# The first stage's pieces in a new order, the first expert weights loaded during it, and gathers spread over the first cross-attention tile

## The chip, the cores and the metric

One core of one Trainium2 chip runs the whole program in one launch. The metric is the device time in microseconds (us) from launch to end; the kernel before was timed three times, and one further execution was recorded by the hardware profiler. TensorE is called PE here, VectorE DVE, ScalarE ACT, GpSimd POOL and SyncE SP.

## The reference

All data is float32. `x` is (32, 32, 512), that is 1024 tokens, 8 tiles of 128; `ctx_1024` is (32, 257, 512), one context of 257 rows for each group of 32 tokens.

```python
x = x + _L0_xattn_ref(_layernorm(x), ctx_1024, ctx_1024, ctx_1024)   # (gelu(x ctx^T) * (x ctx^T)) ctx
x = x + _L0_attn_ref(_layernorm(x), w_qkv, w_proj, q_norm_w, k_norm_w)  # RMS norm, rope, causal, 16 heads
x = x + _L0_ffn_ref(_layernorm(x), gate_w, gate_b, w1, b1, w2, b2)   # 32 experts, top 2, capacity 77
x = x + _L1_xattn_ref(_layernorm(x), ctx_1024, Wq, bq, Wk, bk, Wv, bv, Wo, bo)
x = x + _L1_attn_ref(_layernorm(x), ...)     # group norm, decayed linear attention, SiLU MLP
x = x + _L1_ffn_ref(_layernorm(x), w_freq_real, w_freq_imag, bias)   # ifft(fft(x) @ w), as one real matrix
```

The router of the third line is

```python
probs = softmax(xt @ gate_w + gate_b); top_w, top_i = top_k(probs, 2)
pos_all = cumsum(one_hot(top_i.reshape(-1)), axis=0) - 1   # place of each token within its expert
xe = zeros(E, C, D).at[flat_e, pos_d].add(x_rep, mode='drop')
he = gelu(einsum('ecd,edf->ecf', xe, w1) + b1, approximate=False)
ye = einsum('ecf,efd->ecd', he, w2) + b2
```

## The kernel before

The program is written engine by engine, with semaphores set by hand, and each engine runs its instructions strictly in the order in which they stand. It has three stages.

The first stage (`phase_a`, lines 359 to 378) goes over the 8 tiles. A tile's work is cut into pieces: `gated(i)` is the first line of the reference (layer norm, its transposes at L1361, the products with the context at L1368 and L1384, the next layer norm and its transposes at L1333); `scored(i)` makes queries, keys and values (the 512 wide matmuls of L1323), norms and turns them on DVE (L963 to L979, with a root on POOL at L550), transposes them (L1407) and multiplies them to scores (L1414); `attended(i)` is the softmax, the product with the values (L1427), the projection (L1323) and the third layer norm; `routed(i)` gives the gate's logits (L1323, 32 wide). Each engine has a generator for each piece, and `interleave` strings them by the letters of `PLAN_A` (g, a, z, w for gated, scored, attended, routed), so that several tiles are under way; tiles 2 to 6 are the turns of a hardware loop.

Then `PLAN_B` joins the last tiles with `spectral` (the 257 wide matmuls of L1323, first half of the real matrix of the last reference line, after `folds` on DVE at L945) and with `route(0)`, the router for tiles 0 to 5; `route(1)` does it for tiles 6 and 7. POOL writes the token rows to the experts' places in DRAM by 16 indirect DMAs (L591, the scatter). Behind that PE does a small reordering of biases (L1460) and the second half of the spectral matrix, waits for `m_sb`, transposes the first expert's rows (L1477) and begins the experts.

SP (lines 395 to 540) issues the loads. The weights of an expert are `w1` and `w2`, 4 MiB each, in a ring of two places each; the first stage's own buffers lie in the same memory. Before, SP waited for the last gate matmul (`gate_ps`) and loaded w1 and w2 of expert 0; then it waited for the scatter and loaded the first two experts' rows; then it waited for the spectral matrix and loaded w1 of expert 1.

The second stage is the 32 experts (hidden layer L1488, transposes L1496, result L1506). The third, `phase_c`, goes over the 8 tiles again: `head`, `cross` (cross-attention, 4 contexts a tile: scores L1593, softmax on DVE at L1220 and ACT at L823, transposes L1608, values, keys of the next context), and `tail` (the rest). Ahead of each tile it adds the two gathered expert outputs of every token (`add_expert`, L1166). POOL gathers tile 0 ahead of the stage and the other seven tiles, 14 indirect DMAs, in one row behind the first layer norm (`gather_others`, L664); DVE waits for all of them once and adds them in pieces during tile 0's cross-attention (`other_tiles`, L1295).

## Time and profile before

| what | value |
|---|---|
| median of 3 runs | 2064.54 us (2060.41 to 2065.12) |
| the profiled execution | 2075.67 us |
| its span, first to last instruction | 2073.9 us |
| PE busy | 1934.6 us, 93% of the span |
| DVE, ACT, POOL busy | 704.7, 556.9, 196.9 us |
| mean granted PE clock | 0.970 |
| DMA | 374.95 MB, mean 181 GB/s |

"Busy" is the time in which an engine had an instruction at work. In the rows below a timeline line gives start and length in us, the engine, the line of the kernel, the operation, output<-input, the number of instructions merged, and in brackets the idle time before it with the engine that ended it. The granted clock 1.00 is PE's full 2.4 GHz and 0.50 is 1.2 GHz. The profiled execution lies 11.13 us above the median of the runs. By time the stages are: first stage and routing from 0 to about 336 us, experts to about 1098 us, the rest to the end.

### The profile page before, as it was taken

How to read it: one execution, taken by the hardware profiler on the slowest of the kernel's cores; microseconds unless marked ns; L12 is line 12 of the kernel's file. 1: busy time of each engine (PE TensorE's matmuls, PEld its weight loads, DVE VectorE, ACT ScalarE, POOL GpSimd, SP SyncE). 2: the span in 40 equal slices, each digit the busy share in tenths (PEclk: the TensorE clock that was granted, in tenths of full speed). 3: DMA queues.
4: the chain of work that ended last, by engine and by line, in shares of the span. 5: the costliest groups of instructions: out<-in, count | busy, mean ns of one | idle time of the engine just before them, and what ended most of it. 6: DMA issues, size and time to landing. Idle time of an engine off the chain costs nothing.

```text
span 2073.9 us, 37462 instructions
## 1 busy us (share of the span) xinstructions
PE 1934.6 (93%) x15676; PEld 981.9 (47%) x15676; DVE 704.7 (34%) x1536; ACT 556.9 (27%) x1123; POOL 196.9 (9%) x182
## 2 busy tenths in 40 slices
PE   5789777999999999999996999999999999999977
PEld 2444453333333333333333657565666656575543
DVE  2666671121111211112223433434323333344323
ACT  1333311222222222222211234233333333242321
POOL 1122221000000000000003000000000000000000
PEclk9999988999999999999998999999999999999988
DMA  9643228999999999999976020100000000000000
GB/s 338 221 163 144 79 73 344 396 396 387 382 388 375 380 362 379 379 375 379 367 280 207 22 102 22 27 21 27 12 26 22 21 27 22 17 22 27 11 1 11
DMA packets 86295, 374.95 MB, mean 181 GB/s; under 512 B 7782, under 2 KB 25702, under 8 KB 53432
## 3 DMA queue, kind: packets, MB, share of 16 engines
q1 hardware_dynamic: 79544, 355.71, 44.9%
q0 software_dynamic: 6656, 17.77, 2.4%
q8 instruction: 83, 1.36, 0.3%
q14 instruction: 12, 0.10, 0.0%
HBM read 357.73 MB, written 16.45 MB: 180 GB/s over the span
## 4 chain that ended last, share of the span: by engine, by line
PE 85%; issue 4%; ACT 3%; SPq 3%; DMA 2%; DVE 2%; POOL 1%; another core or an unknown queue 0%; POOLq 0%; DVEq 0%; ACTq 0%
PE ps L1323 38%; PE ps L1506 16%; PE ps L1488 16%; PE ps L1713 3%; PE ps L1496 2%; PE ps L1608 1%; PE ps L1514 1%; DMA arena<-in_ctxT 1%; ACT arena L685 1%; PE ps L1384 1%; PE ps L1593 1%; DMA xe_rows<-arena,uidx 1%; PE ps L1634 1%; SPq L432 1%; PE ps L1477 1%
## 5 line engine op out<-in xcount | busy, mean ns | idle before, releaser
L1323 PE MATMUL ps<-arena 128*128 128x512 f32 (+3 forms) x3120 | 893.6, 442 | 38.0 <-ACT arena L685 10.0
L1323 PEld LDWEIGHTS ps<-arena 128*128 128x128 f32 x3120 | 529.1, 193 | 372.6 <-issue 296.7
L1506 PE MATMUL ps<-arena 128*32 128x512 f32 x3072 | 373.6, 594 | 0.0
L1488 PE MATMUL ps<-arena 128*32 128x512 f32 x3072 | 363.3, 595 | 0.7 <-issue 0.6
L550 POOL TENSOR_TENSOR arena<-arena 128x1 f32<-128x1 f32 (+3 forms) x80 | 129.2, 1615 | 1103.2 <-DVE arena L913 643.7
L1121 DVE COPY arena<-ps 128x512 f32<-128x512 f32 x96 | 66.4, 691 | 482.7 <-PE ps L1506 482.7
L1488 PEld LDWEIGHTS ps<-arena 128*32 128x32 f32 x3072 | 109.3, 109 | 225.4 <-issue 225.4
L1506 PEld LDWEIGHTS ps<-arena 128*32 128x32 f32 x3072 | 100.4, 109 | 198.1 <-issue 195.6
L783 ACT ACTIVATE arena<-ps 128x512 f32<-128x512 f32 x96 | 57.3, 597 | 352.5 <-PE ps L1488 352.5
L813 ACT ACTIVATE arena<-ps,arena 128x257 f32<-128x257 f32 x128 | 60.7, 477 | 202.8 <-PE ps L1323 202.8
L1220 DVE TENSOR_REDUCE arena<-ps 128x1 f32<-128x257 f32 x128 | 54.2, 423 | 122.5 <-PE ps L1593 112.7
L789 ACT ACTIVATE arena<-arena 128x512 f32<-128x512 f32 x96 | 58.3, 631 | 127.2 <-DVE arena L1128 127.1
L607 POOL DMA_DIRECT2D y_rows<-arena x32 | 16.8, 526 | 744.4 <-DVE arena L1136 744.4
L823 ACT ACTIVATE arena<-ps,arena 128x257 f32<-128x257 f32 x128 | 60.6, 476 | 92.7 <-DVE arena L1221 78.1
L830 ACT ACTIVATE arena<-ps 128x512 f32<-128x512 f32 x64 | 34.9, 595 | 172.7 <-PE ps L1608 172.5
L1213 DVE TENSOR_TENSOR arena<-ps,arena 128x512 f32<-128x512 f32 x64 | 43.9, 689 | 76.6 <-PE ps L1323 76.5
L1128 DVE TENSOR_TENSOR arena<-ps,arena 128x512 f32<-128x512 f32 x96 | 60.3, 684 | 20.0 <-PE ps L1496 20.0
L1136 DVE TENSOR_TENSOR arena<-ps,arena 77x512 f32<-77x512 f32 x32 | 22.0, 688 | 117.7 <-PE ps L1514 117.7
L1713 PE MATMUL ps<-arena 128*128 128x512 f32 x128 | 61.5, 625 | 0.0
L1496 PEld LDWEIGHTS ps<-arena 128*128 128x128 f32 x384 | 41.3, 140 | 26.0 <-issue 26.0
L1496 PE MATMUL ps<-arena 128*128 128x128 f32 x384 | 48.9, 277 | 0.0
L1608 PE MATMUL ps<-arena 128*128 128x128 f32 x256 | 34.1, 277 | 13.1 <-DVE arena L1226 13.1
(198 smaller groups left out, 1323.8 us busy)
## 6 DMA issues: line engine op xcount, KB each, us to landing
arena<-in_w SPq DMA_DIRECT2D x64, 4096.0 KB, 13.8
arena<-in_ctxT SPq DMA_DIRECT2D x8, 2056.0 KB, 7.9
arena<-in_ctxT SPq DMA_DIRECT2D x32, 514.0 KB, 3.6
arena<-in_ctx SPq DMA_DIRECT2D x8, 2048.0 KB
xe_rows<-arena SPq DMA_DIRECT2D x8, 616.0 KB
arena<-in_b POOLq DMA_DIRECT2D x32, 154.0 KB, 7.5
arena<-xe_rows SPq DMA_DIRECT2D x32, 154.0 KB
y_rows<-arena POOLq DMA_DIRECT2D x32, 154.0 KB, 6.2
```

The costliest lines, as they stand in the source:

```text
L550: pool.tensor_tensor(dst, src, half_sb[:, 0:src.shape[-1]], ALU.pow).then_inc(done, 1)
L783: act.activation(h_sb[:, t, :].rearrange("p (c f) -> p c f", c=HB), ps[:, t, :].rearrange("p (f c) -> p c f", c=HB), ACT.Copy).then_inc(h_ ...
L789: act.activation(hT[s][:, t], hT[s][:, t], ACT.Gelu).then_inc(hT_rdy, 1)
L813: act.activation(kT_c[:, m, :], ps[:, bK(m), 0:S], ACT.Identity, bias=bk_sb[:, m:m + 1], scale=1.0).then_inc(k_ev, 1)
L823: act.activation(P_c[:, g, 0:S], ps[:, bS(g), 0:S], ACT.Exp, bias=nmx[:, g:g + 1], scale=SCALE, accum_out=smc[:, g:g + 1]).then_inc(exp_c, 1)
L1121: dve.tensor_copy(yp_sb[:, t, :], ps[:, ST + t, :]).then_inc(yp_out, 1)
L1128: TT(hT[s][:, t].rearrange("p c (n u) -> p c n u", n=HB), ps[:, t, :].rearrange("p (c n u) -> p c n u", c=HB, n=HB), bc(b.unsqueeze(3), P, ...
L1323: ins = pe.matmul(dst, lhsT, rhs, start=(n == 0), stop=(n == len(pairs) - 1))
L1488: ins = pe.matmul(ps[q4[n], t, :], xeT[s][:, k, q4[t]], w1_sb[s][:, k, n * D:(n + 1) * D], start=(k == 0), stop=(k == KD - 1))
L1496: ins = pe.transpose(ps[:, t, chunk(c)], h_sb[:, t, chunk(c)], id_sb)
L1506: ins = pe.matmul(ps[q4[n], ST + t, :], hT[s][:, t, c, q4[n]], w2_sb[s][:, n * HB + c, :], start=(c == 0), stop=(c == HB - 1))
L1713: ins = pe.matmul(ps[:, w.b7, :], w.hT2[:, f, :], fw2_sb[:, f, :], start=(f == 0), stop=(f == FT2 - 1))
```

## The change

Four things change together.

1. The first stage gets a new order. The first layer norm and its transposes are cut off `gated` as `lead`, and run two tiles ahead. Values are made ahead of queries and keys; the scores' matmuls move from `scored` to `attended`, behind the next tile's value matmuls. The rope on DVE works on the raw queries and keys, and the root mean square's factor is multiplied in last, so rope no longer waits for POOL. PSUM banks change with it: transposes of queries and keys use banks 4 and 5, the scores bank 3 (6 in the last tile), the routing bank 3 (7 in the last two tiles). `folds` is cut in two parts, one in the last `scored`, one in the last `attended`.
2. The first stage's buffers are laid out so that w1 of expert 0 can be loaded when the last tile's queries and keys are turned (`qkT_rdy`), and w1 of expert 1 and w2 of expert 0 when the last projection is done (`proj_ps`).
3. The bias reordering and the second half of the spectral matrix become a piece `matrix`, which is interleaved with `route(1)`. The first two experts' rows are loaded by POOL, not SP, behind the scatter.
4. The gathers of tiles 1 to 7 are issued in four groups (4, 4, 4 and 2), each when the softmax of one context of tile 0 is done and the group before has landed; DVE adds each tile where it stands in a list.

PE, first stage, the whole order of one turn (the unrolled one of scored(1)), before; L1368 and L1384 are the products with the context, L1323 with 512 columns queries, keys, values and the projection:

```order
L1323 MATMUL ps<-arena 128x512 x12
L1361 MATMUL ps<-arena 128x128 x4
L1368 MATMUL ps<-arena 32x257 x16
L1427 MATMUL ps<-arena 32x128 x16
L1375 MATMUL ps<-arena 128x128 x2
L1375 MATMUL ps<-arena 1x128
L1384 MATMUL ps<-arena 32x512 x12
L1323 MATMUL ps<-arena 128x512 x4
L1407 MATMUL ps<-arena 128x128 x8
L1333 MATMUL ps<-arena 128x128 x4
L1414 MATMUL ps<-arena 32x128 x16
```

and now (L1418 is L1361 of before, L1427 is L1368, L1434 is L1375, L1443 is L1384, L1389 is L1333, L1468 is L1407, L1478 is L1414, L1490 is L1427, L1379 is L1323):

```order
L1379 MATMUL ps<-arena 128x512 x4
L1478 MATMUL ps<-arena 32x128 x16
L1379 MATMUL ps<-arena 128x512 x8
L1427 MATMUL ps<-arena 32x257 x16
L1490 MATMUL ps<-arena 32x128 x16
L1434 MATMUL ps<-arena 128x128 x2
L1434 MATMUL ps<-arena 1x128
L1443 MATMUL ps<-arena 32x512 x12
L1379 MATMUL ps<-arena 128x512 x4
L1389 MATMUL ps<-arena 128x128 x4
L1468 MATMUL ps<-arena 128x128 x8
L1418 MATMUL ps<-arena 128x128 x4
```

The scores stood behind the transposes of their own queries and keys; now the next tile's four value matmuls stand between them. The transposes of `lead` stand last, for the tile after next.

PE, end of the first stage and the way to the experts, before (L1450 are the router's counts, L1460 the bias reordering, L1323 with 257 columns the spectral matrix, L1477 the first expert's rows):

```order
L1450 MATMUL ps<-arena 128x192 x2
L1427 MATMUL ps<-arena 32x128 x16
L1323 MATMUL ps<-arena 128x512 x4
L1323 MATMUL ps<-arena 128x257 x16
L1333 MATMUL ps<-arena 128x128 x4
L1323 MATMUL ps<-arena 128x32 x4
L1450 MATMUL ps<-arena 128x64 x2
L1460 MATMUL ps<-arena 32x128 x16
L1323 MATMUL ps<-arena 128x257 x20
L1477 MATMUL ps<-arena 128x77 x4
```

and now:

```order
L1516 MATMUL ps<-arena 128x192 x2
L1490 MATMUL ps<-arena 32x128 x16
L1379 MATMUL ps<-arena 128x512 x4
L1379 MATMUL ps<-arena 128x257 x16
L1389 MATMUL ps<-arena 128x128 x4
L1379 MATMUL ps<-arena 128x32 x4
L1525 MATMUL ps<-arena 32x128 x16
L1379 MATMUL ps<-arena 128x257 x10
L1516 MATMUL ps<-arena 128x64 x2
L1379 MATMUL ps<-arena 128x257 x10
L1551 MATMUL ps<-arena 128x77 x4
```

The bias reordering and ten of the twenty matmuls now stand ahead of the second counts.

POOL, from the last stores of expert results to the third stage's loop, before (L623 are the gathers, L550 the roots of the layer norms of tiles 0 and 1):

```order
L607 DMA y_rows<-arena 77x512 x2
L623 DMA arena<-y_rows,uidx 128x512 x2
L550 TENSOR_TENSOR arena<-arena 128x1
L623 DMA arena<-y_rows,uidx 128x512 x14
L550 TENSOR_TENSOR arena<-arena 128x1
```

and now:

```order
L623 DMA y_rows<-arena 77x512 x2
L639 DMA arena<-y_rows,uidx 128x512 x2
L558 TENSOR_TENSOR arena<-arena 128x1
L639 DMA arena<-y_rows,uidx 128x512 x8
L558 TENSOR_TENSOR arena<-arena 128x1
L639 DMA arena<-y_rows,uidx 128x512 x6
```

The root of tile 1's layer norm now stands behind the second of the four groups.

The core of the diff:

```diff
-        rA = Region(ring_off[0][0], 2 * RW)
+        rA = Region(ring_off[0][0], RW)
...
+        rA = Region(ring_off[0][1], RW)
...
-        rM = Region(ring_off[1][0], RW)
         KH, HF = KD // 2, D // 2
-        ATr, ATi, tmpM = rM.take(KH, D), rM.take(KH, D), rM.take(2, HD)
+        ATr, tmpM = rM.take(KH, D), rM.take(2, HD)
+        ATi = view(WORDS - KH * D, KH, D)
...
-        PLAN_A = "gzawgawgzgagzaga"
-        PLAN_B = "zwwrmrzzrm"
+        PLAN_A = "hazagawzgawgzagazh"
+        PLAN_B = "wzwrmrzzzrm"
...
+        def bA(i):
+            return 6 if isinstance(i, int) and i == NT - 1 else 3
+
+        def bR(i):
+            return 7 if isinstance(i, int) and i >= NT - 2 else 3
...
+        def phase_a(eng, lead, gated, scored, attended, routed, spectral, my, per, route, matrix):
+
+            run(lead(0))
             run(gated(0))
-            interleave(PLAN_A, a=scored(0), g=gated(1))
-            interleave(PLAN_A, a=scored(1), g=gated(2), z=attended(0))
-            with eng.Fori(2, NT - 1) as i:
+            run(lead(1))
+            interleave(PLAN_A, a=scored(0), g=gated(1), h=lead(2))
+            interleave(PLAN_A, a=scored(1), g=gated(2), h=lead(3), z=attended(0))
+            with eng.Fori(2, NT - 2) as i:
                 if my is not None:
                     my.loop(i, per, 2)
-                interleave(PLAN_A, a=scored(i), g=gated(i + 1), z=attended(i - 1), w=routed(i - 2))
+                interleave(PLAN_A, a=scored(i), g=gated(i + 1), h=lead(i + 2), z=attended(i - 1), w=routed(i - 2))
             if my is not None:
-                my.leave(NT - 1)
+                my.leave(NT - 2)
+            interleave(PLAN_A, a=scored(NT - 2), g=gated(NT - 1), z=attended(NT - 3), w=routed(NT - 4))
             interleave(PLAN_A, a=scored(NT - 1), z=attended(NT - 2), w=routed(NT - 3))
             interleave(PLAN_B, z=attended(NT - 1), w=routed(NT - 2), m=spectral, r=route(0))
             run(routed(NT - 1))
-            run(route(1))
+            interleave("rsrsrs", r=route(1), s=matrix)
...
-            sp.wait_ge(gate_ps, NT)
+            sp.wait_ge(qkT_rdy, 5 * NT)
             load_w1(0, 0)
+            sp.wait_ge(proj_ps, NT)
+            sp.dma_start(w1_sb[1], rows(w1[1])).then_inc(w1_in[1], 16)
             load_w2(0, 0)
-            sp.wait_ge(scattered, 16 * 2 * NT)
-            for s in range(2):
-                load_rows(s, s)
             sp.wait_ge(m_sb, 2 * KD)
...
-            load_w1(1, 1)
...
+            pool.wait_ge(scattered, 16 * 2 * NT)
+            for s in range(2):
+                pool.dma_start(xe_sb[s][0:CAP, :], xe_dram[s * CAP:(s + 1) * CAP, :]).then_inc(xe_first, 16)
...
-            def gather_others():
-                for i in range(1, NT):
-                    gather(i)
-                return {}
-
-            phase_c(pool, head, cross, tail, None, None, gather_others)
+            def other_tiles():
+                yield
+                for b in range(NB):
+                    pool.wait_ge(pn_rdy, (HG + 1) * (b + 1))
+                    if b > 0:
+                        pool.wait_ge(gathered, 32 * 2 * b)
+                    for i in range(2 * b + 1, min(2 * b + 3, NT)):
+                        gather(i)
+                    for _ in range((2, 4, 4, 5)[b]):
+                        yield
+
+            def first_tile():
+                return {"t": other_tiles()}
+
+            phase_c(pool, head, cross, tail, None, None, first_tile)
...
+            def moments(a, src, w=None):
+                stats_rdy = ln_stats[a] if w is None else w.ln_stats
                 dve.drain()
                 dve.bn_stats(stats, src)
                 dve.drain()
                 my.step(dve.bn_aggr(mv, stats))
                 TS(veps, mv[:, 1:2], LN_EPS, None, ALU.add).then_inc(stats_rdy, 1)
+
+            def normed(a, src, dst, n, done=None, w=None):
...
+            def folds(part):
+                even, odd, w, w_in = ((We_r, Wo_r, Wr_sb, Wr_in), (We_i, Wo_i, Wi_sb, Wi_in))[part]
+                dve.wait_ge(w_in, 16)
+                TT(even[:, :, 1:HF], w[:, :, 1:HF], w[:, :, D - 1:HF:-1], ALU.add).then_inc(W_fold, 1)
+                TT(odd[:, :, 1:HF], w[:, :, 1:HF], w[:, :, D - 1:HF:-1], ALU.subtract).then_inc(W_fold, 1)
+                dve.tensor_copy(even[:, :, 0:1], w[:, :, 0:1]).then_inc(W_fold, 1)
+                odd, sign = ((Wo_i, -1.0), (Wo_r, 1.0))[part]
+                TS(odd[:, :, 0:1], w[:, :, HF:HF + 1], sign, None, ALU.mult).then_inc(W_fold, 1)
...
-                my.step(TT(qkn, ps[:, 4:6, :].rearrange("p a (h d) -> p (a h) d", h=H),
-                           bc(rs.unsqueeze(2), P, 2 * H, DH), ALU.mult))
+                yield
                 v4 = "p (a h) d -> p a h d"
-                qn4, A4, B4 = (a.rearrange(v4, a=2) for a in (qkn, ropeA, ropeB))
+                A4, B4 = (a.rearrange(v4, a=2) for a in (ropeA, ropeB))
+                qn4 = ps[:, 4:6, :].rearrange("p a (h d) -> p a h d", h=H)
                 my.step(TT(A4, qn4, bc(CW.unsqueeze(2), P, 2, H, DH), ALU.mult))
                 hd = DH // 2
                 my.step(TT(B4[:, :, :, 0:hd], qn4[:, :, :, hd:DH],
                            bc(SW[:, :, 0:hd].unsqueeze(2), P, 2, H, hd), ALU.mult))
                 my.step(TT(B4[:, :, :, hd:DH], qn4[:, :, :, 0:hd],
                            bc(SW[:, :, hd:DH].unsqueeze(2), P, 2, H, hd), ALU.mult))
-                TT(qkr, ropeA, ropeB, ALU.add).then_inc(qkr_rdy, 1)
-                yield
+                my.step(TT(qkn, ropeA, ropeB, ALU.add))
+                if isinstance(i, int) and i == NT - 1:
+                    folds(0)
+                yield
+                yield
+                dve.wait_ge(rs_rdy, i + 1)
+                TT(qkr, qkn, bc(rs.unsqueeze(2), P, 2 * H, DH), ALU.mult).then_inc(qkr_rdy, 1)
...
+                for _ in range(3):
+                    yield
+                for n, tiles in enumerate(((1,), (2,), (3,), (4,), (), (), (5,), (6,), (), (), (7,), (), ())):
+                    for i in tiles:
+                        dve.wait_ge(gathered, 32 * min(2 * ((i + 1) // 2), NT - 1))
+                        add_experts(i)
+                    if n < 12:
...
+                wait(pe, lg_rdy, i - 2)
                 transposes(1, xn1, i, 3)
...
+                wait(pe, vA_rdy, i)
+                for a in (2, 0, 1):
+                    group(ps[:, 4 + a, :], [(xnT[:, k, :], wqkv0_sb[:, k, a * D:(a + 1) * D]) for k in range(KD)],
+                          qkv_ps if a == 1 else None)
...
+            def matrix():
+                pe.wait_ge(b1_in, 16)
+                b1_fen = b1_sb.rearrange("p e (n f) -> p f e n", f=HB)
+                for c in range(HB):
+                    for f in range(HB):
+                        ins = pe.matmul(ps[q4[f], 6, chunk(c)].rearrange("p (e n) -> p e n", n=HB), id_sb[:, c:P:HB],
+                                        b1_fen[:, f], start=True, stop=True)
+                ins.then_inc(b1_ps, 1)
...
+                    group(ps[:, half, 0:HD], [(ATr[:, k, chunk(m)], C_sb[:, k, :]) for k in range(KH)]
+                          + [(ATi[0:1, 0, chunk(m)], C_sb[0:1, KH, :])])
+                    group(ps[:, half + 1, 0:HD], [(ATi[:, k, chunk(m)], S_sb[:, k, :]) for k in range(KH)], m_ps)
+                    if m == 1:
+                        yield
```

## Rows read from the trace of the kernel before

**Rows 1.** The page's section 4, the chain that ended last, by engine and by line.

```profile
PE 85%; issue 4%; ACT 3%; SPq 3%; DMA 2%; DVE 2%; POOL 1%; another core or an unknown queue 0%; POOLq 0%; DVEq 0%; ACTq 0%
PE ps L1323 38%; PE ps L1506 16%; PE ps L1488 16%; PE ps L1713 3%; PE ps L1496 2%; PE ps L1608 1%; PE ps L1514 1%; DMA arena<-in_ctxT 1%; ACT arena L685 1%; PE ps L1384 1%; PE ps L1593 1%; DMA xe_rows<-arena,uidx 1%; PE ps L1634 1%; SPq L432 1%; PE ps L1477 1%
```

**Rows 2.** Window of one tile: length, busy us (instructions) per engine, clock, DMA share, GB/s.

```profile
121.51:151.21 29.70, 26.21 (x184) 13.38 (x184) 19.08 (x35) 10.44 (x18) 7.03 (x4) 0.96 0.38 142
```

**Rows 3.** Waits of PE from 61 to 240 us: total, times, longest.

```profile
PE ps L1333 <- ACT arena L740: 10.1, 5, 2.0
PE ps L1384 <- ACT arena L720: 4.1, 6, 0.7
```

**Rows 4.** Timeline inside one tile: start, length, operation, count, [idle before <- releaser].

```profile
172.42 3.71 PE L1323 MATMUL ps<-arena 128*128 128x512 f32 x8
...
175.93 0.68 DVE L940 TENSOR_TENSOR arena<-arena,ps 128x512 f32 x1
...
178.48 0.55 DVE L915 TENSOR_SCALAR arena<-arena 128x512 f32 x1 [0.66 <-POOL arena L550]
...
179.17 0.63 PE L1333 MATMUL ps<-arena 128*128 128x128 f32 x4 [2.02 <-ACT arena L740]
```

**Rows 5.** Timeline of the start of the first stage.

```profile
28.05 13.39 PE L1323 MATMUL ps<-arena 128*128 128x512 f32 x24 [2.02 <-DMA arena<-in_wproj0T]
...
32.74 0.69 DVE L910 BATCH_NORM_STATS2 arena<-arena 128x6 f32<-128x512 f32 x1 [7.88 <-DMA arena<-in_x]
...
75.32 3.32 PE L1368 MATMUL ps<-arena 128*32 128x257 f32 x32 [3.11 <-DMA arena<-in_ctxT]
```

**Rows 6.** Timeline of PE at the end of the first stage.

```profile
240.40 11.35 PE L1323 MATMUL ps<-arena 128*128 128x512 f32 x24
...
271.06 1.08 PE L1414 MATMUL ps<-arena 128*32 128x128 f32 x32 [2.56 <-ACT arena L740]
...
301.37 1.08 PE L1323 MATMUL ps<-arena 128*128 128x32 f32 x8 [0.69 <-ACT arena L675]
307.58 1.11 PE L1450 MATMUL ps<-arena 128*128 128x64 f32 x4 [5.13 <-DVE arena L1066]
...
335.18 0.75 PE L1477 MATMUL ps<-arena 77*128 77x77 f32 x4 [6.75 <-DMA arena<-xe_rows]
336.55 4.50 PE L1488 MATMUL ps<-arena 128*32 128x512 f32 x20 [0.62 <-issue]
```

**Rows 7.** Timeline of SP's and POOL's DMA issues there.

```profile
302.90 0.57 SPq L455 DMA_DIRECT2D arena<-in_w  x1
332.38 0.73 SPq L460 DMA_DIRECT2D arena<-xe_rows  x2
...
297.07 1.22 POOL L591 DMA_INDIRECT xe_rows<-arena,uidx  x1 [0.43 <-issue]
...
317.18 0.98 POOL L591 DMA_INDIRECT xe_rows<-arena,uidx  x1 [0.30 <-issue]
```

**Rows 8.** Windows: around the last Q and K, the loads before the experts, the experts.

```profile
252.84:265.95 13.11, 6.95 (x45) 4.32 (x46) 11.41 (x16) 1.54 (x3) 6.33 (x1) 0.61 0.01 1
300.00:330.00 30.00, 18.46 (x90) 11.68 (x88) 13.23 (x55) 2.78 (x7) 14.85 (x16) 0.77 0.96 382
600.00:700.00 100.00, 100.00 (x907) 34.42 (x898) 19.38 (x30) 21.75 (x33) 4.21 (x8) 1.00 0.95 379
```

**Rows 9.** Waits in the opening of the first cross-attention tile.

```profile
DVE arena L1220 <- remote: 9.7, 3, 5.9
```

**Rows 10.** Timeline of PE and POOL there.

```profile
1136.37 1.97 PE L1608 MATMUL ps<-arena 128*128 128x128 f32 x8 [13.05 <-DVE arena L1226]
...
1130.26 0.96 POOL L623 DMA_INDIRECT arena<-y_rows,uidx  x1 [0.30 <-issue]
```

**Rows 11.** The chain that ended last, before that tile.

```profile
1099.24 3.02 DMA y_rows<-arena
...
1104.45 5.22 DMA arena<-y_rows,uidx
```

More of the change, by code:

```diff
@@ L553, in norm_root, with lead @@
                 root(veps, rstd, ln_stats[a], n + 1, ln_rstd[a])
-            def gated(i):
+            def lead(i):
                 norm_root(0, i)
@@ L708, in route, with lead @@
                 yield
-            def gated(i):
+            def lead(i):
                 yield
@@ L1355, in _, with lead @@
             pe.wait_ge(id_in, 16)
-            def gated(i):
+            def lead(i):
                 yield
@@ L1471, in _ @@
+            phase_a(pe, lead, gated, scored, attended, routed, spectral(), None, None, route, matrix())
             pe.wait_ge(m_sb, 2 * KD)
             def rows_in(e, s, i):
-                pe.wait_ge(xe_in[s], 16 * i + 16)
+                if isinstance(i, int) and i == 0:
+                    pe.wait_ge(xe_first, 32)
+                else:
+                    pe.wait_ge(xe_in[s], 16 * i)
                 for k in range(KD):
```

151 lines of the change are left out of this document (76 added, 75 removed).

## Prediction

> **What bounds the kernel now.** I read the chain that ended last first: 85% of it is PE, most in the shared matmul helper and the experts [rows 1]. The experts are closed to this change: in the window from 600 to 700 us PE is busy 100.00 of 100 us at clock 1.00 while DMA is at 0.95 [rows 8], so neither a load that comes sooner nor a buffer that frees sooner shortens them. What is left is where PE stands. A tile of the first stage takes 29.70 us with 26.21 of PE at clock 0.96 [rows 2]; the waits behind the missing time are ACT's copies of the turned keys (10.1 us in five tiles) and ACT's copy of the turned hidden values (4.1 in six) [rows 3]. Then comes a stretch with little PE work and much DMA: the last gate matmul starts at 301.37, the experts at 336.55 [rows 6], and from 300 to 330 us DMA is at 0.96 with 382 GB/s [rows 8]. Third, in the opening of the first cross-attention tile DVE waits 9.7 us in three pieces for a release the profile puts on no engine of the core [rows 9], and PE is idle 13.05 us before 1136.37 [rows 10]; POOL's 14 gathers are issued until 1131.2 beside that [rows 10].
>
> **The start** loses 2.5 us. Today queries, keys and values of tile 0 start at 28.05, before the other tiles of x have landed; the layer norm of tile 1 starts at 32.74 when they have [rows 5]. In the new order PE stands at tile 1's transposes first. Norm 2.4 us (the 3.1 from addition to normalised in rows 4, less the addition), transposes 1.1, copy 0.6: the matmuls start at about 36.6, 8 us late. But PE also waits 3.11 us for the context of tile 2 at 75.32 [rows 5], a DMA time which stays, since SP's order up to there does not change. Walking the pieces of tiles 0 and 1 through (13.4 for the three products as in rows 5, the products with the context, DVE's norm, the rest at 3.5 us a product) I come to 77.8 for tile 2's context product: 2.5 late.
>
> **The tiles** gain 23 us, so 20.5 in all by the last one. With the value matmuls of the next tile (3.6 us, from 3.71 for eight instructions [rows 4]) and the transposes of lead (0.6) between the turning of the keys and the scores, ACT's 3.0 us of copies are covered; the hidden values' copy is covered by the values' product and the gate. What can be late next is DVE's norm behind the gated product: addition to normalised in 3.1 us (175.93 to 179.03 [rows 4]), and now the factor of rope, about 1.2 us (twice the 0.68 of a product half as wide), stands in it, filling the 0.66 us wait for POOL: 3.75 us, against the projection of 3.55 and hand-over; PE waits some 0.3. DVE itself has about 19 busy us in a tile [rows 2], and rope's wait for POOL's root is gone. So a tile takes PE's own work, 26.21 us x 0.96 = 25.2 at full clock, plus 0.3 plus some 0.5 for hand-overs: 26.0. From 77.8: the rest of that turn 12.7, four turns of 26.0, and one without lead of 25.4, and the last tile's products start at 219.9, today 240.40 [rows 6].
> Bounds: 25.2 is the floor (4 us more); at 28 us a tile, one more hand-over of 2.02 as today's longest [rows 4], it is 10 less.
>
> **The last tile** gains 4 us and gives 1 back. Today the scores of tile 7 start 30.7 us after its products (271.06 [rows 6]), since folds sits ahead of the rope and the root takes 6.33 [rows 8]. Now: products and tile 6's scores 11.6, ACT's square 1.0, then DVE. Its 11.41 us of that stretch [rows 8] lose half of folds (2.6), and the root runs beside them: 9.4 with gaps. Transposes 1.4, copies 3.0: 26.4. From there to the gate today takes 30.3 us (301.37). The other half of folds now stands ahead of the softmax: I take 31.5, with 0.7 of it for PE at clock 0.5 after its idle time before the counts, as in the 0.61 window of rows 8. The gate starts at 277.8, 23.5 us early.
>
> **The way to the experts** gains 6 us more. Weights: w1 of expert 0 is issued near 246 and has landed by 258. w1 of expert 1 and w2 of expert 0 follow the last projection at 269.6; that is 8.4 MB, and 16 scatters of 128 rows are 4.2 MB. At 395 GB/s, a little over the 382 of rows 8, 12.6 MB take 32 us: 301.6. The scatter: the second batch's indices come 11.5 us behind the gate (today 10.5 to 11, with the counts at 307.58 [rows 6]; ten spectral matmuls and the biases, 5.4 us, stand ahead of them now, and DVE needs 4.9 for its part anyway, so 0.5 late), its four issues end at 294.6, at a pace of 1.28 (297.07 to 317.18 for 15 [rows 7]). Today the last issue is at 317.18 and the rows' load begins at 332.38 [rows 7], 15 us later, when all loads have drained. Both ways end near 302, DMA bound. Rows: POOL's two loads at 3.02, as the store of an equal piece [rows 11], and 0.6 for the second: 305.6. Today SP's take 2.80 (332.38 to 335.18). Then 1.37 as today (335.18 to 336.55): experts at 307.0. Gain over 336.55: 29.5 us. The second half of the spectral matrix ends about 292, under the scatter; if it were not covered it would cost its 5 us. The experts themselves gain nothing.
> The Trainium skill ("DMA: Bandwidth & Descriptors", on the anatomy of one DMA from gpsimd) gives about 2.0 us plus bytes over 436 GB/s, an estimate of 2.4 us for these rows; the store in rows 11 is 0.6 longer, and by the page the sum would be 0.6 better.
> The same page (queues, rings and completion order) says that a DMA engine goes round between its queues, packet by packet. Then the scatter would not stand behind the weights but share with them; 15 us in rows 7 speak for a share too small to matter, and by the rule alone, with 5.2 us for an indirect DMA [rows 11] behind 294.6, the experts would begin 2 us earlier.
> Bounds: 5.2 us behind the last issue gives 299.8, 2 better; at 330 GB/s the bytes take 38 us, 6 worse.
>
> **The gathers** gain 5 us, between -5 and 9.7. Tile 0's opening needs nothing of the other gathers. If the 9.7 us of rows 9 are theirs, they go. What they are is not shown: matmuls are recorded as done, their release comes late. DVE's new waits are not late: a group is issued at the end of a softmax (5.1 us for four), lands 5.2 later [rows 11], and its first addition stands behind value products of 7 us and a layer norm of 2.6. Against the full 9.7: each group now flies beside PE's matmuls, and the profiled execution is 11.13 us over the median, so part of 9.7 may belong to it alone. If the groups hold PE for the share of today's flight (9.7 of about 23 us from the first issue to 1136.37), four flights of 10 us cost 15, a net loss of 5. I take half of 9.7.
>
> **Sum.** Against the profiled execution: 2075.67 - 29.5 - 5 = 2041; it lies 11.13 above the median, and the steps carry over as they are: 2064.54 - 34.5 = 2030.0 us.
>
> **Rivals.**
> A, the forecast: 2030, own range 2024 to 2037. Chance 0.48.
> B, the whole hold goes in unprofiled runs too: 2064.5 - 29.5 - 9.7 = 2025. For it: nothing else is late there. 0.17.
> C, DMA takes the gain of the way to the experts and the hold is only in the profile: 29.5 - 6 and nothing from the gathers, 2041. For it: 12.6 MB from 269.6; against: 382 GB/s at the same mix today. 0.17.
> D, the tiles stay chained at 28 us: 34.5 - 10, 2040. For it: DVE's norm has 0.3 us too little room already. 0.10.
> E, slower: indirect DMAs in flight hold PE. Place: the 16 scatters now fly from 272 to 302 beside the last projection, gate and counts, and the gathers, 36 us, beside cross-attention. At today's worst share, 9.7 of the 14.3 us from the scores to 1136.37, 66 us cost 45: 2064.5 - 29.5 + 45 - 9.7 = 2070. It decides from a share of about 0.6. Against: today's scatters run beside matmuls, and the last gate and counts wait for ACT and DVE alone [rows 6]. 0.04.
> Between these, about no change: 0.04.
>
> About 0.3%, 6 us, is what a measurement of this kernel can tell from no change. A to D are all faster by more: 0.92; same 0.04; slower 0.04. The range: 2018 takes in B with tiles at their floor, 2044 takes in C and D.
>
> **What would show it.** In the new profile: tile 2's context product near 78; turns of 26 us with PE at clock 1.00 and no wait for ACT's key copies; last products at 220, last gate at 278; two weight loads issued at 270 and DMA full to 302; first expert matmul at 307 and from there PE busy without a gap, as before; the gap before the first transposes of cross-attention at 3 to 4 us instead of 13.05. Wrong would be: a turn of 28 with PE waiting for DVE's norm, experts at 313 with DMA still full, or new late releases beside each group of gathers.

## The result, and the profile after

| | before | changed |
|---|---|---|
| median of 7 runs, us | 2060.41 (2059.38 to 2065.12) | 2053.86 (2045.44 to 2055.52) |
| ratio to before, 95% interval | | 0.9944 [0.9933, 0.9955] |
| profiled execution, us | 2075.67 | 2053.86 |
| its span, us | 2073.9 | 2052.3 |

Forecast were 2030.0 and a range of 2018 to 2044. The kernel became faster, but by much less than the 34.5 us forecast: the two medians differ by 6.6 us (0.32%), the median of 2064.54 from which the forecast started lies 10.7 us above the new time, and the ratio of the table says 0.56%, 11.5 us. That is a fifth to a third of the forecast. The time lies 10 us outside the range.

**The first stage went as predicted.** The windows of two tile turns and of 100 us of the experts, after: length, busy us (instructions) of PE, PEld, DVE, ACT and POOL, clock, DMA share, GB/s.

```profile
116.49:141.99 25.50, 24.79 (x185) 12.37 (x184) 19.45 (x35) 10.51 (x18) 7.96 (x5) 1.00 0.44 166
167.56:193.09 25.53, 24.82 (x185) 12.40 (x184) 19.45 (x35) 10.54 (x18) 7.99 (x5) 1.00 0.45 165
...
600.00:700.00 100.00, 100.00 (x911) 35.09 (x913) 21.59 (x33) 23.14 (x35) 4.20 (x8) 1.00 0.93 374
```

A turn takes 25.5 us instead of 29.70 [rows 2], with the same PE work at clock 1.00. PE's waits from 61 to 220 us:

```profile
PE ps L1389 <- DVE arena L953: 8.2, 7, 4.2
PE ps L1443 <- ACT arena L747: 0.6, 1, 0.6
```

The 10.1 and 4.1 us of waiting for ACT [rows 3] are 0.6 in all; what is left is a wait for DVE's norm, 4.2 us of it once, in tile 1, and else about 0.6 a turn (0.58 in the turn shown next) where 0.3 was expected. The timeline of PE from the start of the stage to the experts (start, length, operation, count, [idle before <- releaser]):

```profile
77.41 1.95 PE L1427 MATMUL ps<-arena 128*32 128x257 f32 x32
...
89.11 0.65 PE L1389 MATMUL ps<-arena 128*128 128x128 f32 x4 [0.58 <-DVE arena L953]
...
218.02 3.68 PE L1379 MATMUL ps<-arena 128*128 128x512 f32 x8
...
244.04 1.94 PE L1478 MATMUL ps<-arena 128*32 128x128 f32 x32
...
277.78 1.08 PE L1379 MATMUL ps<-arena 128*128 128x32 f32 x8 [0.69 <-ACT arena L700]
...
286.04 0.55 PE L1516 MATMUL ps<-arena 128*128 128x64 f32 x4
...
305.26 0.75 PE L1551 MATMUL ps<-arena 77*128 77x77 f32 x4 [4.22 <-DMA arena<-xe_rows]
306.63 6.10 PE L1562 MATMUL ps<-arena 128*32 128x512 f32 x28 [0.62 <-issue]
```

These answer to [rows 5, 6]: context product of tile 2 at 77.41 (forecast 77.8), last tile's products at 218.02 (219.9), the last gate product at 277.78 (277.8), experts at 306.63 (307.0; before 336.55). The DMA issues there, which answer to [rows 7]; the last one is the load of the first two experts' rows:

```profile
294.74 0.97 POOL L603 DMA_INDIRECT xe_rows<-arena,uidx  x1 [0.30 <-issue]
301.72 1.19 POOL L614 DMA_DIRECT2D arena<-xe_rows  x2 [6.02 <-DMA xe_rows<-arena,uidx]
```

The experts keep their pace, and the first cross-attention tile opens without the long hold of [rows 10]: its transposes wait 3.27 us instead of 13.05.

```profile
1090.54 0.73 PE L1667 MATMUL ps<-arena 32*32 32x257 f32 x32 [1.25 <-DVE arena L1264]
...
1095.54 1.97 PE L1682 MATMUL ps<-arena 128*128 128x128 f32 x8 [3.27 <-DVE arena L1281]
```

**The third stage gave most of it back.** Each of its 32 contexts begins with 32 matmuls of scores (L1667; L1593 before), and L1674 (L1600 before) opens a tile. From the starts of these, in us:

| | first scores | opening of tile 1 to that of tile 7 | from there to the end |
|---|---|---|---|
| before, first profile | 1120.4 | 687.6 | 176.5 |
| before, second profile (e12_before_again, below) | 1118.1 | 684.7 | 176.7 |
| changed | 1090.5 | 705.4 | 176.4 |

Six turns with the same instructions take 18 to 21 us longer. The loss sits between the first scores of a tile and those of its second context, in tiles 2 to 6: 24.6 to 26.5 us where the kernel before takes 21.6. PE there, changed kernel, timeline:

```profile
1393.75 3.70 PE L1379 MATMUL ps<-arena 128*128 128x512 f32 x8 [0.69 <-ACT arena L706]
1397.88 0.64 PE L1667 MATMUL ps<-arena 32*32 32x257 f32 x8 [0.43 <-issue]
1400.89 0.81 PE L1667 MATMUL ps<-arena 32*32 32x257 f32 x24 [2.38 <-issue]
1401.63 5.24 PE L1379 MATMUL ps<-arena 128*128 128x512 f32 x8
```

PE stops after eight of 32 identical matmuls that nothing in the kernel separates, for 2.38 us, released by "issue": no engine and no DMA of the kernel. The eight projections behind it take 5.24 us instead of 3.71: the granted clock has fallen. PE's longest waits from 1200 to 1900 us, first those of the changed kernel, then those of the kernel before:

```profile
PE ps L1667 <- issue: 13.1, 7, 2.6
PE ps L1379 <- ACT arena L710: 6.5, 12, 0.9
PE ps L1379 <- ACT arena L706: 4.1, 6, 0.7
```

```profile
PE ps L1323 <- ACT arena L685: 6.5, 12, 0.9
PE ps L1323 <- ACT arena L681: 4.1, 6, 0.7
PE ps L1593 <- issue: 0.2, 1, 0.2
```

The waits for ACT agree to the digit; "issue" has grown from 0.2 to 13.1 us. (The changed kernel has 0.9 us of waits for DVE besides, but e1_pad_after below has them too and does not lose.) The clock does not fall behind every stop. The windows of two such starts, the first with clock 1.00, the second with 0.93:

```profile
1280.40:1305.00 24.60, 22.20 (x179) 13.23 (x180) 13.01 (x33) 5.84 (x16) 3.84 (x2) 1.00 0.11 34
1397.90:1424.10 26.20, 23.82 (x179) 13.83 (x180) 12.77 (x33) 5.83 (x16) 3.84 (x2) 0.93 0.10 32
```

The five turns with a stop take 117.2, 119.1, 119.3, 118.7 and 117.2 us. In the three long ones the trace has one stretch of 3.41 us each at granted clock 0.50 (at 1401.3, 1520.8 and 1640.3), in the other two none. So a turn pays about 3.1 us for the stop and, in three of five, 1.4 to 2.1 more for the clock.

The queue "instruction" brings an engine its program. It moved 83 packets in the first profile of before and 90 in this one, 1.47 MB, so 16 KB each:

```profile
q8 instruction: 90, 1.47, 0.3%
```

In the trace none of these packets flies from 400 to 1000 us, so the experts' loop runs from what PE holds. In the third stage they come in every turn, ten of them (nine before), and three stand in a row around the loop's turn: 1392.4, 1395.4 and 1398.4 us, the last of them half a microsecond after the eighth load has started (1397.9). The ninth load starts at 1400.9. PE's branch instruction at the loop's end takes 3.3 to 3.9 us in the third stage in both kernels, and 0.2 in the first stage's loop and the experts'. So the suspect was the loop's place in the program's memory: the first stage is written out for one tile more, and 372 more TensorE instructions stand ahead of the third stage's loop (counted in the program, an f32 matmul as two loads and two matmuls, as the trace has it; the records of the two traces, with each loop taken once, differ by 374).

The Trainium skill ("Runtime: NRT & Kernel Launch", on instruction fetch mechanics) says that blocks are 16 KB, 256 instructions, that they are fetched ahead in sequence, and that a taken branch to a block outside the window forces a fetch before execution goes on. The trace agrees on the 16 KB and on the branch, which takes 3.86 us from 1393.86 while a packet flies from 1395.4; the 256 are tested below. How large the window is the trace shows from one side only: the experts' loop of 886 instructions branches back 13 times with no packet.

### The profile page after: what moved, and what is told of

Its sections match the earlier page's. It is cut to its first block, busy times and chain, and to the rows that moved or that the text cites. A ratio compares the mean times of both kernels' runs of the same rounds, so it can differ in the third digit from the quotient of the medians.

```text
span 2052.3 us, 37446 instructions
## 1 busy us (share of the span) xinstructions
PE 1932.3 (94%) x15676; PEld 978.3 (48%) x15676; DVE 704.7 (34%) x1536; ACT 556.1 (27%) x1123; POOL 203.2 (10%) x184
## 3 DMA queue, kind: packets, MB, share of 16 engines
q8 instruction: 90, 1.47, 0.3%
## 4 chain that ended last, share of the span: by engine, by line
PE 87%; DVE 4%; issue 3%; ACT 2%; DMA 2%; POOL 1%; SPq 1%; DVEq 0%; POOLq 0%
PE ps L1379 38%; PE ps L1580 17%; PE ps L1562 16%; PE ps L1787 3%; PE ps L1570 2%; PE ps L1682 1%; PE ps L1588 1%; PE ps L1443 1%; ACT arena L710 1%; DMA arena<-in_x 1%; PE ps L1667 1%; POOL arena L558 1%; PE ps L1708 1%; PE ps L1389 1%; PE ps L1551 1%
## 5 line engine op out<-in xcount | busy, mean ns | idle before, releaser
L1379 PE MATMUL ps<-arena 128*128 128x512 f32 (+3 forms) x3120 | 893.6, 442 | 27.8 <-ACT arena L710 9.9
L1379 PEld LDWEIGHTS ps<-arena 128*128 128x128 f32 x3120 | 528.8, 193 | 356.1 <-issue 285.5
L558 POOL TENSOR_TENSOR arena<-arena 128x1 f32<-128x1 f32 (+3 forms) x80 | 134.6, 1683 | 1031.0 <-DVE arena L948 556.8
L818 ACT ACTIVATE arena<-ps 128x512 f32<-128x512 f32 x96 | 57.3, 597 | 353.2 <-PE ps L1562 353.2
L623 POOL DMA_DIRECT2D y_rows<-arena x32 | 16.8, 526 | 730.6 <-DVE arena L1191 730.6
L865 ACT ACTIVATE arena<-ps 128x512 f32<-128x512 f32 x64 | 34.8, 595 | 183.6 <-PE ps L1682 183.5
L1570 PE MATMUL ps<-arena 128*128 128x128 f32 x384 | 48.9, 277 | 0.0
L700 ACT ACTIVATE arena<-ps 128x512 f32<-128x512 f32 x32 | 19.1, 597 | 86.3 <-PE ps L1389 75.0
```

Of the source, the lines that this page charges most:

```text
L558: pool.tensor_tensor(dst, src, half_sb[:, 0:src.shape[-1]], ALU.pow).then_inc(done, 1)
L818: act.activation(h_sb[:, t, :].rearrange("p (c f) -> p c f", c=HB), ps[:, t, :].rearrange("p (f c) -> p c f", c=HB), ACT.Copy).then_inc(h_ ...
L1379: ins = pe.matmul(dst, lhsT, rhs, start=(n == 0), stop=(n == len(pairs) - 1))
L1570: ins = pe.transpose(ps[:, t, chunk(c)], h_sb[:, t, chunk(c)], id_sb)
```

## Experiments

Twelve kernels, in two groups. The table has the medians of the timed ones; "before" is the kernel before, timed beside them on the same chip. The columns of the third stage are read from each trace: which load of a tile's scores the stop stands behind, and the five turns from tile 1 to tile 6.

| kernel | median, us | before | ratio, 95% interval | stop behind load | five turns, us |
|---|---|---|---|---|---|
| e1_pad_after | 2038.06 | 2064.68 | 0.9881 [0.9867, 0.9896] | none | 573.6 |
| e2_pad_before | 2088.33 | 2064.68 | 1.0121 [1.0107, 1.0136] | 8 | 591.6 |
| e3_unrolled | 2031.07 | 2064.68 | 0.9841 [0.9829, 0.9854] | none | 568.9 |
| e4_gathers_at_once | 2053.74 | 2064.68 | 0.9935 [0.9921, 0.9949] | as changed | 593.9 |
| e5_before_unrolled | 2063.65 | 2064.68 | 0.9991 [0.9981, 1.0001] | none | 570.5 |
| e6_pad60_before | 2068.27 | 2064.68 | 1.0020 [1.0009, 1.0030] | 36 (three turns of five) | 574.5 |
| e7_late_weights | 2045.22 | 2064.68 | 0.9905 [0.9885, 0.9924] | none | 568.9 |
| e8_pad30_after | 2032.39 | 2064.68 | 0.9859 [0.9837, 0.9880] | none | 573.8 |
| e9_pad12_after | 2056.15 | 2065.23 | 0.9958 [0.9945, 0.9972] | 2 | 591.5 |
| e10_pad18_after | 2034.13 | 2065.23 | 0.9854 [0.9839, 0.9869] | none | 573.6 |
| e11_pad88_before | 2082.87 | 2065.23 | 1.0090 [1.0076, 1.0104] | 22 | 591.7 |

For comparison: before 573.7 and 570.7 (its two profiles), changed 591.4 and a stop behind load 8.

### The place of the loop

**e1_pad_after** adds instructions that only wait, two satisfied waits in each, at the head of TensorE's program:

```diff
         def _(pe):
+            for _ in range(2 * 140):
+                pe.wait_ge(x0_in, 16)
```

> The changed kernel with 140 instructions that only wait for x's first tile, long satisfied, put ahead of everything on TensorE. TensorE idles there until 28 us, so they cost it nothing by themselves; what they change is where every later instruction lies in the program's memory. Theory 1 (the lost 17 us are TensorE's instruction fetch at the back edge of the third stage's loop): the changed kernel's loop head lies about 16 instructions before the end of a 16 KB block, so that after the branch it runs 8 loads of scores (L1667) and stands 2.4 us for the next block, six times, and each stop drops the clock behind it; with 140 more instructions ahead the head lies as far from the block's end as in the kernel before, the stop behind the eighth load goes, a turn is 114 to 116 us instead of 117 to 119, and the time is 2036 to 2040. Theory 2 (the turns are longer because of what the change did to the data side: spread gathers, queue order, tiles' places): nothing moves, 2054. Theory 3 (a state of the chip in that one profile): the turns fall in the profile but the time stays 2054.

Measured 2038.06, and the turns are nearly those of the first profile of before: 114.0, 115.7, 115.7, 114.0, 114.2 (there 114.0, 115.7, 115.7, 114.2, 114.1). The place of stop and clock drop above, in e1_pad_after, timeline, and ahead of it the projections in front of the first scores, for two turns:

```profile
1276.50 3.70 PE L1381 MATMUL ps<-arena 128*128 128x512 f32 x8 [0.69 <-ACT arena L706]
...
1390.53 5.40 PE L1381 MATMUL ps<-arena 128*128 128x512 f32 x8 [0.69 <-ACT arena L706]
1395.86 0.71 PE L1669 MATMUL ps<-arena 32*32 32x257 f32 x32
1396.51 3.71 PE L1381 MATMUL ps<-arena 128*128 128x512 f32 x8
```

All 32 matmuls go through, and the eight projections behind them take 3.71 us again. The first two lines also tell the turns of 114.0 from those of 115.7: the second line is of a turn of 115.7, and from 1390.7 to 1394.1 the granted clock is 0.51, so that the same eight projections take 5.40 us instead of 3.70. In every profile with no stop the turns of 115.5 us and more hold just one such stretch, and the shorter ones none. 140 instructions that do nothing made the changed kernel 16 us faster; the data side of the change is untouched, so theory 2 falls, and with the time moving as the profile does, theory 3 too.

**e2_pad_before** is the counter-test, 116 such instructions in the kernel before (same edit with 116).

> The kernel before with 116 instructions that only wait, long satisfied, ahead of everything on TensorE: this puts the head of its third-stage loop where the changed kernel has it, with nothing else of the change. Theory 1 (instruction fetch): its turns grow from 114 to 116 us to 117 to 119, with 2 to 2.6 us of waiting inside the first scores of a turn, so 2060 becomes about 2075 (2070 to 2078). Theory 2 (the data side of the change): no difference, 2060.

```profile
1432.39 0.64 PE L1595 MATMUL ps<-arena 32*32 32x257 f32 x8
1434.35 0.70 PE L1595 MATMUL ps<-arena 32*32 32x257 f32 x24 [1.33 <-issue]
```

The stop appears in the kernel before, behind the same eighth matmul (1.33 us in the turn shown, 2.38 to 2.65 in the other four). 372 more instructions ahead and 116 more ahead put the loop in the same place; they differ by 256. The turns cost 17.9 us more than in the first profile of before, as expected. The time rose by 23.6, more than my upper end of 2078: my expectation took the pads for free until 28 us, but PE's first transposes start at 8.18 us in before, here at 16.33. At the experts 4.06 us of it were left; 17.9 + 4 explain 22 of the 23.6. Against the second profile of before the same two terms are 20.9 and 5.5, so 23.6 lies between.

**e9_pad12_after** and **e10_pad18_after** (the edit with 12 and 18 in the changed kernel) differ by six instructions, one on either side of the block's end by my count.

> The changed kernel with 12 waiting instructions ahead on TensorE. If the stop is where the block with the loop's head ends, 17 instructions behind the head less these 12, it now stands behind the second load of scores instead of the eighth, at the same length: turns 117 to 120 us, time 2052 to 2058. If instead any shift off the changed kernel's place helps, 2035 to 2048.

> As e9_pad12_after with six waiting instructions more, 18. The end of the block now lies in front of the loop's head instead of behind it, so the block that the branch asks for holds all of the scores. Theory of the place: no stop in the scores, turns 114 to 116 us, 2032 to 2037: about 20 us from e9_pad12_after by six instructions that do nothing. If what counts is a distance in blocks that changes slowly with the place, the two differ by less than 3 us.

```profile
1399.69 0.59 PE L1669 MATMUL ps<-arena 32*32 32x257 f32 x2 [0.45 <-issue]
1402.70 0.72 PE L1669 MATMUL ps<-arena 32*32 32x257 f32 x30 [2.42 <-issue]
```

2056.15 and 2034.13: six idle instructions are worth 22 us. Twelve instructions (six loads, six matmuls) moved the stop from the eighth load to the second, in the timeline above, which is of e9_pad12_after. **e8_pad30_after** puts the loop's head 12 further:

> The changed kernel with 30 waiting instructions ahead on TensorE instead of the 140 of e1_pad_after. The loop's head then lies at the start of a block, with about 243 instructions to its end. Theory 1: no stop in the scores, turns 114 to 115.7 us, time 2036 to 2038, about 2 us less than e1_pad_after since fewer waits are carried through the start. If instead more instructions ahead were what helps, 30 of them would give back a fifth of what 140 did: 2051.

2032.39, no stop. Few instructions are as good as many; only the place counts.

**e6_pad60_before** and **e11_pad88_before** (60 and 88 in the kernel before) ask where in the scores a stop hurts.

> The kernel before with 60 waiting instructions ahead on TensorE. By theory 1 a turn's cost hangs on how many instructions lie between the loop's head and the end of its 16 KB block: 133 in the kernel before (turns 114.0 to 115.7), 17 with 116 ahead (117.3 to 120.0). With 60 ahead it is 73: all 64 load and matmul instructions of the scores go through before the stop, and what stands behind it is work that nobody waits for at once. So the stop costs less than in e2_pad_before: turns of 115 to 117 us, time 2065 + 2 (the waits' own, half of the 4 that 116 cost) + 5 to 10, 2072 to 2077. If only the number of added instructions mattered (a cost in proportion), it would be half of e2_pad_before's 23.6: 2077. If it is the place alone with a threshold that lies above 73 instructions: as e2_pad_before, 2083.

> The kernel before with 88 waiting instructions ahead on TensorE: the block's end lies 45 instructions behind the loop's head, so the stop should stand behind the 22nd of the 32 loads of scores (in e6_pad60_before it stood behind all 32 and four more loads, cost 1.3 to 1.6 us in three turns of five and no more). The last scores are needed by the softmax, which everything behind waits for, so I expect the full price again: turns of 117 to 120 us, time 2080 to 2086 (2065 + 3 for the waits at the start + 15 to 18). If a stop costs less the later in the scores it comes, as the work behind it shrinks, 2070 to 2078.

First e6_pad60_before, then e11_pad88_before:

```profile
1421.41 0.73 PE L1595 MATMUL ps<-arena 32*32 32x257 f32 x32
1422.07 1.99 PE L1325 MATMUL ps<-arena 128*128 128x512 f32 x4
1424.62 0.70 PE L1325 MATMUL ps<-arena 128*128 128x512 f32 x1 [0.56 <-issue]
```

```profile
1426.56 0.69 PE L1595 MATMUL ps<-arena 32*32 32x257 f32 x22 [0.16 <-issue]
1429.49 0.65 PE L1595 MATMUL ps<-arena 32*32 32x257 f32 x10 [2.23 <-issue]
```

28 instructions moved the stop by 14 loads, 36 to 22, exactly. Behind load 36 it lies under work that PE already has queued: 0.56 us, turns 574.5 in all, and I expected too much (2072 to 2077; 2068.27). Inside the scores it costs the full price wherever it stands, 591.7, as expected (2082.87).

**e3_unrolled** takes the back edge away on TensorE alone:

```diff
-            with eng.Fori(1, NT - 1) as i:
-                ...
+            if eng is nc.tensor:
+                for i in range(1, NT - 1):
+                    interleave(PLAN_C, c=cross(i, True), t=tail(i - 1, one), h=head(i + 1))
+            else:
+                with eng.Fori(1, NT - 1) as i:
+                    ...
```

> The changed kernel with TensorE's loop of the third stage written out (six turns one behind the other, no back edge; the other engines keep their loops). Theory 1: without a taken branch the stream of blocks is read straight on; both the 3.3 to 3.9 us that the loop's branch takes in the trace and the stop behind the eighth load of scores go. Turns as in the kernel before or shorter, 113 to 115.5 us, and the time 2030 to 2038. Theory 2: the turns stay at 117 to 119 us and the time at 2054.

2031.07. All turns are 113.8 us and the queue "instruction" moves 75 packets. **e5_before_unrolled** is the same edit in the kernel before, so that the pair shows the change without the loop's place in it.

> The kernel before with TensorE's loop of the third stage written out, as in e3_unrolled. With it both sides of the change are without the back edge, so that the change can be measured by itself: the trace says that what it moves ahead of the third stage starts 29.9 us earlier. Theory 1: this kernel gains only the 4.8 us by which its five whole turns (573.7 us) exceed those of e3_unrolled (568.9): 2060 where the kernel before has 2065, and e3_unrolled is 29 to 31 us under it. If the change had lost anything beyond the fetch in the third stage, the difference would be smaller.

2063.65: the unrolling is worth 1 us there, which the interval does not tell from nothing, and not 4.8; the first profile of before has two stretches at the low clock in its five turns, this one has one and e3_unrolled none, and each costs 1.7. The pair differs by 32.6 us (2063.65 - 2031.07; they ran on two chips, on both of which before took 2064.68), where 29 to 31 were expected. In their profiles 31.2 of it stand ahead of the first scores (1121.7 and 1090.5): the change lost nothing in the third stage but the fetch.

### The gathers and the weights

**e4_gathers_at_once** undoes the gathers on GpSimd:

```diff
-            def other_tiles():
-                ...
+            def gather_others():
+                for i in range(1, NT):
+                    gather(i)
+                return {}
...
-                        dve.wait_ge(gathered, 32 * min(2 * ((i + 1) // 2), NT - 1))
+                        if i == 1:
+                            dve.wait_ge(gathered, 32 * (NT - 1))
```

> The changed kernel with GpSimd's 14 late gathers issued at once again behind the opening tile's head, as in the kernel before (VectorE waits for all of them before its first addition); the first stage, the early weights and VectorE's places for the additions stay as changed. If the gathers hold up the opening scores' semaphores, the 9.7 us hold comes back in the profile: 11 us between the scores' end and the transposes instead of 5. If that hold is there in every execution the time is 2054 + 10 = 2064; if the hold shows in a profiled execution alone, as the 15 us between the profiled execution and the median of the kernel before suggest, 2054 (2052 to 2057) with a profiled execution about 10 above. If the gathers hold nothing, neither moves. The third stage's turns stay at 117 to 119 us by every theory but that which blames the spread gathers for them (then 114 to 116, 2037).

```profile
1090.50 0.73 PE L1659 MATMUL ps<-arena 32*32 32x257 f32 x32 [1.25 <-DVE arena L1255]
...
1095.62 1.97 PE L1674 MATMUL ps<-arena 128*128 128x128 f32 x8 [3.40 <-DVE arena L1272]
```

2053.74 against 2053.86, ratios 0.9935 and 0.9944 with intervals that overlap: no worth of spreading the gathers shows, and issued at once they hold nothing. **e12_before_again** asked whether the hold belongs to that program.

> The kernel before once more, unchanged, for a second profile of it. The first profiled execution took 2075.67 us and held PE for 13.05 us ahead of the opening tile's transposes; four profiles with all gathers at once in other variants (e2, e4, e5, e6) held it for 3 us. If that hold belongs to one execution, this profile has a span of 2062 to 2066, scores at about 1120 and transposes 5 us behind them. If it belongs to this very program, the span is 2074 again.

```profile
1118.14 0.73 PE L1593 MATMUL ps<-arena 32*32 32x257 f32 x32 [1.25 <-DVE arena L1209]
...
1123.14 1.97 PE L1608 MATMUL ps<-arena 128*128 128x128 f32 x8 [3.28 <-DVE arena L1226]
```

Its span was 2058.9 us (2060.54 with what lies around it), 3 below the range I gave; the hold is gone. Seven profiles with the gathers at once (before twice, e2, e4, e5, e6, e11) show it once, in the very one that the prediction was read from.

**e7_late_weights** is e3_unrolled with the experts' first loads back in their old place:

```diff
-            sp.wait_ge(qkT_rdy, 5 * NT)
-            load_w1(0, 0)
-            sp.wait_ge(proj_ps, NT)
-            sp.dma_start(w1_sb[1], rows(w1[1])).then_inc(w1_in[1], 16)
+            sp.wait_ge(gate_ps, NT)
+            load_w1(0, 0)
             load_w2(0, 0)
             sp.wait_ge(m_sb, 2 * KD)
+            sp.dma_start(w1_sb[1], rows(w1[1])).then_inc(w1_in[1], 16)
```

> e3_unrolled (2031) with the experts' first weights loaded as late as in the kernel before: w1 and w2 of expert 0 after the last gate product (277.8 us), w1 of expert 1 after the matrix of the spectral part (301). The new order of the first stage stays. By the prediction's own working (the rows wait until all bytes of weights and scatter have drained) the loads end near 309 instead of 302 and the experts start 5 to 7 us later, 312 to 314: 2036 to 2038. Rival: only the last scatter sets the rows' time and DMA shares out evenly, so the weights' place is worth nothing: 2031, experts at 307. Opposite: fewer bytes beside the scatter let the rows come sooner, but w1 of expert 1 comes too late for its first matmul: 2030 to 2034 with a new wait of TensorE for w1 near 330.

```profile
295.48 0.97 POOL L606 DMA_INDIRECT xe_rows<-arena,uidx  x1 [0.30 <-issue]
308.48 1.19 POOL L617 DMA_DIRECT2D arena<-xe_rows  x2 [12.03 <-DMA xe_rows<-arena,uidx]
```

```profile
317.05 0.75 PE L1554 MATMUL ps<-arena 77*128 77x77 f32 x4 [15.27 <-DMA arena<-xe_rows]
318.42 13.10 PE L1565 MATMUL ps<-arena 128*32 128x512 f32 x96 [0.62 <-issue]
```

2045.22 (2037.78 to 2050.07), 14.2 us above e3_unrolled: about twice the 5 to 7 expected, or more. The last scatter is issued at about the same time, 295.48, but POOL's wait for it is 12.03 us instead of 6.02, and the rows come 8.6 us behind their issue (308.48 to 317.05) instead of 3.5 (301.72 to 305.26): w1 of expert 1, issued at 303.02 here, flies beside them. The experts start at 318.42, 11.4 later than in e3_unrolled (307.05), and the first scores come 11.4 later too (1101.9 for 1090.5). Another 3.1 us of the difference between the two profiles lie behind the opening of tile 7 (178.4 for 175.3), and no run explains them. So of the 29.9 us by which the experts start earlier some 11 belong to the weights' place and the rest to the new order, whose parts no run takes singly.

## Why the prediction was wrong

**The start, the tiles, the last tile: right, the last to the digit by luck.** 77.41 for 77.8; turns of 25.5 for 26.0; 218.02 for 219.9; the gate at 277.78 for 277.8. The mechanism named (PE's value matmuls cover ACT's copies, DVE's norm is late next) is in the waits. The tiles came 1.9 us earlier than forecast, and from the last products to the gate it took 59.8 us instead of 57.9: the two errors cancel. In the start the terms listed give 36.8 for the first matmuls of tile 0, the text has 36.6, and they came at 35.93.

**The way to the experts: right in its end, 306.63 for 307.0.** The sum by bytes (weights and scatter drained at 301.6) met the measured 301.72, and from 300.0 to 301.7 us the DMA share is down to 0.15; e7_late_weights, where the rows' load is issued at 308.48 and near 309 was expected, bears out its mechanism. What I priced too low was the share of the early weights: by my bytes they save 5 to 7 us, the experts' start in e7_late_weights says 11.4. Some 5 of this is the rows' own load, 8.6 us instead of 3.5, with a weights' load of 4 MiB issued 5.5 us ahead of it.

**The gathers: the mechanism was wrong.** I took half of a 9.7 us hold as theirs. It belonged to one execution and had nothing to do with them (e4, e12). The doubt was on record ("part of 9.7 may belong to it alone"), but a term whose cause no row showed got half its size where its own bounds reached zero. The forecast was 5 us too low by it. Its lower bound was miscounted as well: four flights of 10 us at a share of 9.7 in 23 cost 17, not 15, a net loss of 7.

**The step that failed is the last one, "the steps carry over as they are".** With it went "the experts themselves gain nothing" and, beyond them, no word on the third stage but its gathers: I took it as unchanged, since no instruction of its loop is. The change moved it all the same. 372 instructions more on TensorE ahead of it put the loop's head 17 instructions before the end of a 16 KB block instead of 133; from then on PE stopped 2.4 to 2.7 us in the scores of five tiles, and in three of the five turns it had a stretch at clock 0.50: 591.4 us for five turns, against 573.7 and 570.7. That is 18 to 21 us. Rivals A to E were all about data; none had the program itself in it.

The account, from the second profile of before (span 2058.9) to the changed one (2052.3): first scores 27.6 earlier, opening to tile 1 0.6 longer (80.0 for 79.4), six turns 20.7 longer, the end 0.3 shorter: -27.6 + 0.6 + 20.7 - 0.3 = -6.6, which is the difference of the spans. Of the 20.7 us the stops make 15.3 (five turns of 117.2 for 570.7) and the low clock 5.4. Without the stop the change does what was forecast: 2031.07 (e3_unrolled) and 2032.39 (e8_pad30_after), 32 to 34 us under the kernel before on the same chips (29 to 33 by the ratios). That 2030.0 comes so near to them is partly luck: the 5 us of the gathers did not exist, and the pair e5 and e3 gave 3 more than the 29.5 of the first stage.

## What to carry to other kernels

In this kernel a loop of 1860 instructions on TensorE was fetched anew at every turn, one of 886 was not. What the fetch costs hangs on where the loop's head lies in the program: an edit far ahead of it, or six instructions that do nothing, moved the time by 1%. So count the instructions that a change adds ahead of such a loop, look for "issue" inside a run of equal matmuls and at the "instruction" queue, and before judging an edit by a per cent compare it with the loop written out on that engine, or at a second place.

A wait that no row explains is worth a second profile before it gets a term; here it was in one of seven. And a load is best moved out of the time in which a small transfer, late and waited for, has to share the engines with it.

## What the runs showed of the hardware

- The block of instruction fetch is 256 instructions here: places 256 apart behave alike (372 and 116 more ahead; 372 + 140 = 512 and none), and the stop moves by one load for each two instructions, over 12, 28 and 28 instructions.
- TensorE's loops of 380 and 886 instructions (first stage, experts) run without any fetch once they are in; that of 1860 fetches nine or ten blocks a turn. In the small ones the branch takes 0.2 us, in the large one 3.3 to 3.9, nearly all of it under matmuls already queued.
- The second block behind the branch's target comes 0.9 to 2.7 us of idle PE later where the first holds 5, 17 or 45 instructions from the loop's head on. Where it holds 73, the fetch is hidden but for about half a microsecond; at 133 and 243 no wait for "issue" at the scores is longer than 0.35 us.
- A satisfied waiting instruction costs about 110 ns on TensorE: with 60, 88, 116 and 140 of them ahead its first matmul starts at 10.29, 13.23, 16.33 and 19.00 us. 30 of them move nothing (8.18 us as without), since PE waits for DVE there anyway.
- A turn of 115.7 us differs from one of 114.0 by one stretch of 3.41 us at granted clock 0.50. Open is why the clock falls in one turn and not in the next at the same place of the loop (e1, e8, e10, and the first profile of before, but not the second), and what held DVE's release for 9.7 us in that one execution.
